# Gated cross attention and mixture of experts on one core: five moves in the engine queues, and router columns repeated 4 times instead of 12

## The reference

```python
x = x + tanh(g_xattn[0]) * attention(layernorm(x), ctx_1024)   # 16 heads of 16, 77 keys
x = x + tanh(g_ffn[0]) * moe(layernorm(x))                      # 8 experts, top 2
...
logits = x2 @ router_w                       # [2048, 8]
top_p, top_e = top_k(softmax(logits), 2)
h = gelu(xd @ w_in[e] + b_in[e])             # per chosen pair (token, expert)
y = (h @ w_out[e] + b_out[e]) * sp
out = zeros.at[st].add(y)
```

## Time and profile before

| | us |
|---|---|
| median of 3 runs | 276.29 |
| lowest and highest | 276.13, 279.11 |
| the profiled execution, its own time | 275.26 |
| its span in the profile | 273.4 |
| TensorE busy | 237.6 (87%) |
| VectorE busy | 166.2 (61%) |
| GpSimd busy | 143.6 (53%) |
| ScalarE busy | 134.9 (49%) |

### The profile page before, as it was taken

How to read it: one execution, slowest core, us unless ns; L and a number is a source line. 1 busy time by engine, 2 the same in 40 slices (tenths; PEclk the granted TensorE clock), 3 DMA queues, 4 the chain that set the end, 5 groups by cost and what they waited for, 6 DMA issues and landing times.

```text
span 273.4 us, 5539 instructions
## 1 busy us (share of the span) xinstructions
PE 237.6 (87%) x1644; PEld 187.0 (68%) x1644; DVE 166.2 (61%) x512; ACT 134.9 (49%) x306; POOL 143.6 (53%) x181
## 2 busy tenths in 40 slices
PE   7899989995699999989688689999999999999900
PEld 4575543653367465734576489999999999999800
DVE  3897957973286548669658026585435343457745
ACT  4347444711771873165314055666566665656520
POOL 3689327327875760003867754444477774446520
PEclk9999999999799999999889979999999999999985
DMA  7910950292233010000222555534353373797365
GB/s 211 340 53 4 448 185 7 78 324 83 77 115 115 17 63 0 2 0 35 82 78 78 154 162 164 161 115 119 118 170 115 106 212 119 223 363 264 116 204 181
DMA packets 25837, 37.34 MB, mean 137 GB/s; under 512 B 3497, under 2 KB 22954, under 8 KB 25714
## 3 DMA queue, kind: packets, MB, share of 16 engines
q1 hardware_dynamic: 21074, 19.91, 24.2%
q0 software_dynamic: 3744, 10.24, 10.4%
q10 hardware_dynamic: 992, 6.84, 7.3%
HBM read 24.64 MB, written 18.39 MB: 157 GB/s over the span
## 4 chain that ended last, share of the span: by engine, by line
PE 48%; POOL 14%; DVE 12%; issue 11%; DMA 10%; ACT 3%; ACTq 0%; POOLq 0%; SPq 0%; DVEq 0%
PE pA L1293 10%; PE pG L1293 9%; PE pM L1293 9%; POOL y_rows L603 8%; DMA stage<-in_w_out 4%; PE pM L1361 4%; PE pA L1622 2%; PE pA L1413 2%; POOL slots L595 2%; PE pA L1399 2%; PE pA L1654 2%; ACT prob L692 2%; PE pA L1419 2%; DVE st L875 2%; POOL rstd L491 2%
## 5 line engine op out<-in xcount | busy, mean ns | idle before, releaser
L603 POOL DMA_INDIRECT y_rows<-y_sb,dst_i x46 | 46.0, 1000 | 40.2 <-ACT y_sb L838 35.9
L1233 DVE TENSOR_TENSOR hT_lo<-pA,hT_hi 128x256 fp32r<-128x256 f32 x46 | 19.5, 424 | 44.3 <-ACT hT_hi L832 44.1
L919 DVE TENSOR_REDUCE mx<-pM 128x4 f32<-128x308 f32 x64 | 27.6, 471 | 21.5 <-PE pM L1361 20.8
L595 POOL DMA_INDIRECT slots<-z2a,pos_u x16 | 16.0, 998 | 29.9 <-DVE pos_u L1133 25.7
L825 ACT ACTIVATE h_sb<-pM 128x256 f32<-128x256 f32 x46 | 17.6, 383 | 23.2 <-PE pM L1293 23.2
L1293 PE MATMUL pM<-win_hi,xT_hi 128*128 x92 | 26.6, 289 | 0.0
L1293 PE MATMUL pM<-win_lo,xT_hi 128*128 x92 | 26.5, 288 | 0.0
L1293 PE MATMUL pM<-win_hi,xT_lo 128*128 x92 | 26.4, 287 | 0.0
L1293 PE MATMUL pA<-wout_hi,hT_lo 128*128 x92 | 25.9, 282 | 0.0
L1293 PE MATMUL pA<-wout_lo,hT_hi 128*128 x92 | 25.9, 281 | 0.0
L1293 PE MATMUL pA<-wout_hi,hT_hi 128*128 x92 | 25.9, 281 | 0.0
(11 more groups left out here) (255 smaller groups left out, 657.1 us busy)
## 6 DMA issues: line engine op xcount, KB each, us to landing
xg<-slots SPq DMA_DIRECT2D x46, 128.5 KB, 2.4
slots<-in_empty ACTq DMA_DIRECT2D x1, 3983.5 KB, 14.8
x_sb<-in_x SPq DMA_DIRECT2D x4, 512.0 KB, 7.1
stage<-in_w_in SPq DMA_DIRECT2D x8, 256.0 KB, 2.7
stage<-in_w_out SPq DMA_DIRECT2D x8, 256.0 KB, 2.6
slots<-in_empty ACTq DMA_DIRECT2D x1, 1927.5 KB, 8.0
yc<-y_rows SPq DMA_DIRECT2D x6, 256.0 KB, 4.5
out<-x_sb SPq DMA_DIRECT2D x6, 256.0 KB, 2.2
```

What stands on the lines that cost most here:

```text
L595: pool.indirect_dma_start(out=slots[GROUP[s]], out_offset=bass.IndirectOffsetOnAxis(ap=pos_u[:, s, q:q + 1], axis=0), in_=z2[int(s > 0)][: ...
L603: pool.indirect_dma_start(out=y_rows[int(j >= JB)], out_offset=bass.IndirectOffsetOnAxis(ap=dst_i[:, j:j + 1], axis=0), in_=y_sb[:, j % YR ...
L919: nc.vector.tensor_reduce(dst[:, 2 * g:2 * g + 2, 2 * h:2 * h + 2], pM[:, g, 0:4 * KV].rearrange("p (r s n) -> p r s n", s=2, n=KV), AX_X, ...
L1233: nc.vector.tensor_tensor(hT_lo[:, j % 2, :], pS[:, 1, 0:D], hT_hi[:, j % 2, :].bitcast(F32), ALU.subtract).then_inc(h_lo, 1)
```

## The change

Seven edits:

1. REP goes from 12 to 4: the products of `logits` have 32 columns and not 96. Their number stays.
2. On GpSimd, `inv_std(0, 3)` and `inv_std(1, 0)` stand behind unit 1 of the expert weights, and not behind unit 3.
3. On ScalarE, `norm2(0)` stands behind `exp(1, 5)`, and not ahead of `exp(1, 3)`.
4. On VectorE, the choice, count and placing of stage 0 stand ahead of `residual(2)`, and not behind it.
5. On TensorE, `ranks(0)` stands behind `scores(3, 0)` and not behind `scores(3, 1)`; it writes to pM in place of pG, so it waits for the last maximum to be read and not for `x1_ready`.
6. TensorE waits for `rank_taken` ahead of `scores(3, 1)`, which writes to pM; `project(3, 1)` no longer waits for it.
7. Three filler products of 512 columns stand behind `transpose_x(0)`, and two behind `transpose_x(1)`.

```diff
-REP = 12
+REP = 4
...
-        pR = [pG, pS, pG]
+        pR = [pM, pS, pG]
...
-            split_weights(0, 4)
+            split_weights(0, 2)
             inv_std(0, 3, var1, rstd1)
             inv_std(1, 0, var2, rstd2)
-            split_weights(4, 12)
+            split_weights(2, 12)
...
                 split_q(b + 1, 0)
-                if b == 1:
-                    norm2(0)
...
                 exp(b, 5)
+                if b == 1:
+                    norm2(0)
...
-            residual(2)
             choose(0, 0)
             choose(0, 1)
             count_first()
             place_pairs(0)
+            residual(2)
...
-                        pe.wait_ge(rank_taken, 1)
                         pe.wait_ge(x1_ready, 3)
...
                 if n == 0:
-                    pe.wait_ge(x1_ready, 3)
+                    pe.wait_ge(sm_red, 16 * BLOCKS)
...
             scores(3, 0)
+            ranks(0)
             scores_rest(3, 0)
             denominators(3, 0)
+            pe.wait_ge(rank_taken, 1)
             scores(3, 1)
-            ranks(0)
...
             transpose_x(0)
+            keep_busy(pA[:, 3, :], w_hi[0], 3)
             transpose_x(1)
+            keep_busy(pA[:, 3, :], w_hi[0], 2)
```

## The result

The changed kernel takes 269.13 us (median of 4 runs, 268.37 to 269.63) against 277.45 before (4 runs, 276.13 to 279.11). The ratio is 0.9695, with a 95% interval from 0.9625 to 0.9765. The profiled execution took 269.63, its span 267.2; the span before was 273.4, so 6.2 us have to be found.

A forecast was written before the change was run, and what follows sets the result against it. The prediction saw a long TensorE program with a few holes, the largest through the expert weights in block 1. Terms 5.7 + 0 + 0.3 + 1.3 = 7.3 us gave 268.5 us, with an 8-in-10 range from 266.4 to 271.6.

The forecast's parts named there:

- The hole in block 1: Block 1, edits 2 and 3: TensorE's 5.28 us wait for an exponential closes, gaining 5.7 us (4.66 to 5.9).
- in a tie: Block 1: norm2(0) done near 70.4, the transposes needing it ready at 70.25 to 70.45, equal within 0.2 us.
- The columns: Logits, edit 1: fewer columns save 0 us (range 0 to 2), since loading 128 columns of weights sets the pace.
- the rival with a chance of 0.13: Thin logits: TensorE's clock falls, about 1.75 us each; total 270.2 with one fall, 272.0 with two; chance 0.13.
- half clock in block 1: Sign of being wrong: TensorE's clock at half speed in blocks 1 and 2.
- the choice of 0 as the whole effect of edit 1: Logits: the sum counted 0 us for the column cut and left a clock fall to a rival.
- The choice ahead of the residual: VectorE, edits 4 to 6: places ready 3.7 us earlier, but only 0.3 us gained (0 to 0.4).
- The filler at the first tiles: First expert tiles, edit 7: filler products on TensorE gain 1.3 us, from 0.5 lost to 1.75 won.
- the step from more work on TensorE to a full clock: First expert tiles: filler in TensorE's waits avoids half speed, which costs two tiles 1.2 to 1.75 us.
- The price of a fall: First expert tiles: two tiles' products and transposes at half speed cost 1.2 to 1.75 us.
- first expert tile loaded near 147.5: Sign of being right: the first expert tile's load comes near 147.5 us; before 146 would be a sign of being wrong.
- The sum: Whole kernel: 5.7 + 0 + 0.3 + 1.3 = 7.3 us gained, giving 268.0 to 269.0, taken as 268.5.

The follow-up runs named there:

- the moved sends: Changed kernel with inv_std(1, 2) and inv_std(1, 3) later among GpSimd's sends, and 8 filler products, not 16, ahead of the first turn of x: 265.77 us, ratio 0.9618.
- REP 4 alone: The kernel before with only REP cut from 12 to 4: 277.01 us over ten runs against 275.45, ratio 1.0049.
- the choice undone: The changed kernel with edits 4 to 6 taken back: 268.99 us, beside the changed kernel at 269.62; ratio 0.9718 to the kernel before.

## Why the prediction was right or wrong

The forecast was 268.5 us, with a range from 266.4 to 271.6; it is 269.13. The parts, by its own steps:

**The hole in block 1: right.** `scores_rest(1, 1)` was to start at 66.14 and did at 66.05; `denominators(1, 1)` at 67.65, and did at 67.55; the transposes between 70.25 and 70.45, and did at 70.16. `norm2(0)` was to be done at 70.4, in a tie, and was at 69.93. 5.7 us was the term; 6.00 was there at the logits. The prediction said that edits 2 and 3 "must be read together", and gave them one price; the runs say more: each does the whole alone. The 5.28 us needed both the late deviation and the order on ScalarE.

**The columns: right in the time of the products, wrong in what follows.** 1.71 us for 1.70. (The recorded 0.12 and 0.13 us for a pass count the tail of the last one too; from start to start it is 0.11 in both.) But the rival with a chance of 0.13, the clock behind the thin logits, came true once, for 1.4 us; it had been priced at 1.75. The prediction had named half clock in block 1 as a sign of being wrong, and it came. The step that failed is the choice of 0 as the whole effect of edit 1. Of seven profiles with REP 4 five have a fall behind `logits(0)` or `logits(1)` (four in `project(1, 1)`, one in `project(2, 1)`); of six with REP 12 none has. Two kernels were profiled with both: the changed kernel (5.23 us twice against 3.73) and that with the moved sends (5.23 against 3.73); the kernel before shows no difference in this place (3.74 and 3.73). So that thin logits make a fall there likelier, for 1.4 to 1.5 us, is shown as a matter of frequency; what decides in a single execution is not. How much of it reaches the total is open: 0.7 us of it was left at the first turn of x with the moved sends, and the ten runs of REP 4 alone don't show where their loss lies.

**The choice ahead of the residual: right.** 0.3 us was the term, and undoing the edits showed 0.29. That GpSimd's queue holds the early sends back is seen in its row (3.67 us idle behind the third send), and that idle time was gone when the two inverse deviations moved on.

**The filler at the first tiles: wrong.** The term was 1.3 us, and in the changed kernel it is 0. The products were hidden as worked out, but the step from more work on TensorE to a full clock failed: with five filler products there the clock fell on the first tile and not on the second. The price of a fall was too high as well: about 1.0 us lies between the profiles with one and those without (8.8 against 7.7 to 8.1). Whether the filler makes it rarer stays open. The sign "first expert tile loaded near 147.5" missed by 1.0 us, which is the fall in `project(1, 1)` less what the hole gave beyond its term: it was loaded at 148.52.

**The sum.** 6.0 at the logits, less 1.4 for the clock, plus 0.3 for the choice, 0 for the filler and about 0.1 in the sends make 5.0 at `second(0)`; 0.4 came in the steady stretch of the experts and 0.8 in the last steps through HBM, which no term had. So the total is near the forecast partly by luck: 7.3 forecast, 6.2 measured in the span, of which 1.2 belongs to no edit (other profiles of the same stretches spread by as much: 95.95 to 96.35 us in the one, 8.9 to 9.8 in the other).

## What to carry to other kernels

When an engine's queue holds a step that isn't urgent ahead of one that is, look for the slack on both sides: here either the supplier's order or the consumer's alone closed a hole of over 5 us, and the second edit added nothing. A result that is ready earlier is worth what the next queue does with it: 3.7 us earlier positions gave 0.3 us, and 3.5 once the sending queue was reordered and the filler behind it shortened as well. Don't take columns out of a product that is no faster for it: here the slow clock came behind the thin product and never behind the wide one. And read a change of a fraction of a microsecond from the starts of the same instructions, not from the total.

## What the runs showed of the hardware that was not expected

The passes of the float32 products keep their pace from 96 down to 32 columns (1.70 and 1.71 us for 16, with 128 columns of weights each), so in this range the pace is not set by the columns streamed.

The granted clock falls at places that the program makes likely but doesn't fix: two kernels with the same program up to there (the changed kernel and the one with the choice undone) had 0.58 and 1.00 of full speed at 77 to 81 us. At `project(3, 1)`, behind an idle TensorE of 2.1 to 2.4 us, it fell in ten of eleven profiles, and in neither of the two in which the wait was filled but for 0.3 and 0.5 us. One fall cost 1.4 to 1.5 us there.

The same kernel took 275.5 us on one chip and 285 on two others. In the kernels profiled there the difference lies in eight expert tiles, 25.8 to 27.8 us against 17.1, in which ScalarE starts up to 2.5 us after the product that it needs is done, for nothing that the profile shows.
